# A fused attention and feed-forward kernel: turned blocks cross memory in one write and eight reads, fp8 steps walk rows with gaps, small vector operations go tile by tile

## The reference

```python
x = x + L0_xattn(layernorm(x), ctx)     # softmax((ctx Wq + bq)(ctx Wk + bk)^T), applied to x
x = x + L0_ffn(layernorm(x))            # rms norm, int8 activations, ternary weights, silu gate
x = x + L1_xattn(layernorm(x), ctx)     # 16 heads, 8 key heads; softmax(q k^T / sqrt(128)) v, then Wo
x = x + L1_ffn(layernorm(x))            # weights rounded to fp8 e4m3, silu gate, scales
```

## Time and profile before

| | |
|---|---|
| median of three runs | 310.96 us |
| the profiled execution | 312.58 us |
| its span, first to last instruction | 310.5 us |
| granted TensorE clock, mean share | 0.995 |
| PE / DVE / ACT / POOL busy | 95% / 84% / 82% / 70% |
| transfers | 44.59 MB, 144 GB/s on average |

### The profile page before, as it was taken

One profiled execution on the slowest core, in us unless ns is written; L12 is line 12 of the kernel. 1 busy time (PEld: TensorE's weight loads), 2 busy tenths in 40 slices (PEclk: granted clock), 3 DMA queues, 4 the chain that ended last, 5 costly groups with the idle time before them and its releaser, 6 DMA issues.

```text
span 310.5 us, 6396 instructions
## 1 busy us (share of the span) xinstructions
PE 293.6 (95%) x1980; PEld 259.9 (84%) x1992; DVE 260.9 (84%) x713; ACT 253.7 (82%) x603; POOL 218.5 (70%) x290
## 2 busy tenths in 40 slices
PE   3968999999999999999999999999999999999994
PEld 2755487798989998979889999999988999899884
DVE  3959999999999999889999986997768897675665
ACT  2398995598999998979999899778899999855460
POOL 3558864556998578999879998886678798952001
PEclk9979999999999999999999999999999999999999
DMA  7996032001326548885878756537645647200103
GB/s 223 367 381 199 35 101 70 1 8 30 93 47 189 157 138 251 220 212 139 228 210 226 199 144 174 161 108 219 182 144 148 179 143 211 68 3 0 36 1 101
DMA packets 54609, 44.59 MB, mean 144 GB/s; under 512 B 11696, under 2 KB 45104, under 8 KB 54576
## 3 DMA queue, kind: packets, MB, share of 16 engines
q1 hardware_dynamic: 54016, 43.93, 49.0%
q10 hardware_dynamic: 560, 0.26, 0.3%
HBM read 27.01 MB, written 15.20 MB: 136 GB/s over the span
## 4 chain that ended last, share of the span: by engine, by line
PE 59%; DVE 20%; DMA 8%; issue 5%; SPq 4%; ACT 2%; DVEq 0%
PE pb L2016 41%; DMA block_room<-blocks 5%; PE pb L2279 5%; PE pb L2314 4%; DMA wraw<-in_wgvT 3%; DVE blocks L1581 3%; SPq L442 2%; DVE sm L1564 2%; PE pb L2130 2%; PE pb L2091 2%; PE pb L2076 2%; DVE wraw L1455 2%; DVE step L1601 1%; PE pb L2227 1%; DVE q_lo L1551 1%
## 5 line engine op out<-in xcount | busy, mean ns | idle before, releaser
L667 POOL TENSOR_TENSOR tp_lo<-tp,pT_hi 128x512 fp32r<-128x512 f32 x54 | 70.0, 1311 | 15.1 <-ACT pT_hi L993 14.8
L981 ACT ACTIVATE sm<-sm,smin 128x256 f32<-128x256 f32 x128 | 63.6, 501 | 4.7 <-DVE smin L1564 4.4
L1564 DVE CUSTOM_DVE_ANT_0 sm<-pb,mask_all 128x256 f32<-128x256 f32 x128 | 47.3, 418 | 5.6 <-PE pb L2016 5.5
L1581 DVE STREAM_TRANSPOSE blocks<-sm 128x1024 f32<-128x1024 f32 x27 | 33.5, 1240 | 7.4 <-DMA block_room<-blocks 7.0
L2016 PE MATMUL pb<-ctx_hi,q_hi 128*128 128x256 f32 x128 | 38.1, 298 | 1.1 <-DVE q_lo L1551 0.6
L662 POOL TENSOR_SCALAR sm<-sm,srec 128x256 f32<-128x256 f32 x64 | 30.5, 488 | 10.4 <-DVE srec L1570 10.4
L2016 PE MATMUL pb<-xT_hi,m_hi 128*128 128x256 f32 x128 | 37.3, 292 | 0.3 <-DVE xT_lo L1540 0.3
L2016 PE MATMUL pb<-n_hi,oT_hi 128*128 128x256 f32 x128 | 37.1, 290 | 0.2 <-DVE oT_lo L1595 0.2
L2016 PE MATMUL pb<-xT_hi,m_lo 128*128 128x256 f32 x128 | 36.2, 283 | 0.0
L2016 PE MATMUL pb<-xT_lo,m_hi 128*128 128x256 f32 x128 | 36.2, 283 | 0.0
L2016 PE MATMUL pb<-ctx_lo,q_hi 128*128 128x256 f32 x128 | 36.2, 282 | 0.0
(11 more groups left out here) (195 smaller groups left out, 943.0 us busy)
## 6 DMA issues: line engine op xcount, KB each, us to landing
block_room<-blocks SPq DMA_DIRECT2D x108, 128.0 KB, 2.8
tp<-block_room SPq DMA_DIRECT2D x54, 256.0 KB, 3.0
w_raw<-in_w SPq DMA_DIRECT2D x4, 576.0 KB, 4.6
wraw<-in_wgvT SPq DMA_DIRECT2D x4, 512.0 KB, 8.4
wraw<-in_woutT SPq DMA_DIRECT2D x2, 512.0 KB, 9.3
out<-xb SPq DMA_DIRECT2D x4, 256.0 KB, 2.2
xa<-in_x SPq DMA_DIRECT2D x3, 256.0 KB, 4.5
xb<-in_ctxT SPq DMA_DIRECT2D x2, 256.0 KB, 5.1
```

What stands on the lines that cost most here:

```text
L667: g.tensor_tensor(tp_lo[:, z, c, :], tp[:, z, c, :], as_f32(pT_hi[:, c, :]), ALU.subtract).then_inc(pT_lo_pool, 1)
L981: a.activation(sm[:, n % 2, k, :], sm[:, n % 2, k, :], ACT.Exp, bias=smin[:, n % 2, k:k + 1], scale=-1.0, accum_out=ssum[:, n % 2, k:k + 1 ...
L1564: v.tensor_tensor_reduce(out=sm[:, n % 2, k, :], in0=bank(passing_bank("s", 2 * n + h))[:, (k % 2) * S:(k % 2 + 1) * S], in1=mask_all[:, b ...
L1581: v.transpose(blocks[:].rearrange("p g k b -> p k g b"), sm[:, n % 2, :, :].rearrange("p k (g b) -> p k g b", b=32)).then_inc(blocks_done, 1)
```

## The change

One DMA now writes all of `blocks` to `block_room` as it lies, 128 partitions with 4 KB each, in place of four DMAs that regrouped it on the way out in runs of 512 bytes. Regrouping moves to the reads: eight DMAs of 32 partitions and runs of 512 bytes (four for each half of `tp`), in place of two of 128 partitions and runs of 2 KB. The counts of the semaphores follow. `sum8` becomes three rows of 96 in rows of 97, and all fp8 steps on both engines see their operands as three rows of 96; VectorE's first step writes into `sum8` and its second reads that. In `stats`, `variances`, `second_stats` and `scaled` the 128x2 instructions become two of 128x1, and two products of tensors become a product with a per-row scalar.

```diff
-        sum8 = tile(ctx, "sum8", [P, PIECE])[:]
+        sum8 = tile(ctx, "sum8", [P, 3, PIECE // 3 + 1])[:, :, 0:PIECE // 3]
...
-        block_room = nc.dram_tensor("block_room", [2 * S, 2 * TOK], F32).ap()
+        block_room = nc.dram_tensor("block_room", [2, P, S * 2 * TOK // P], F32).ap()
...
+        def thirds(piece):
+            return piece.rearrange("p (a n) -> p a n", a=3)
...
-                    sp.wait_ge(blocks_in[0], 16 * (k - 1))
-                    sp.wait_ge(blocks_in[1], 16 * (k - 1))
-                rows = block_room[k % 2 * S:(k % 2 + 1) * S, :].rearrange("(g a) e -> a g e", a=32)
-                for i in range(4):
-                    sp.dma_start(rows[:, :, i * P:(i + 1) * P], blocks[32 * i:32 * (i + 1), :, :, :].rearrange("a g k b -> a g (k b)")).then_inc(blocks_out, 16)
+                    sp.wait_ge(blocks_in[0], 64 * (k - 1))
+                    sp.wait_ge(blocks_in[1], 64 * (k - 1))
+                sp.dma_start(block_room[k % 2], blocks[:].rearrange("p g k b -> p (g k b)")).then_inc(blocks_out, 16)
...
-                sp.wait_ge(blocks_out, 64 * (k + 1))
+                sp.wait_ge(blocks_out, 16 * (k + 1))
+                room = block_room[k % 2].rearrange("(i a) (c g e) -> a c g i e", a=32, c=SC, e=P)
                 for c in range(SC):
                     if k >= 1:
-                        sp.wait_ge(blocks_in[c], 16 * k)
-                    sp.dma_start(tp[:, k % 2, c, :], block_room[k % 2 * S + c * P:k % 2 * S + (c + 1) * P, :]).then_inc(blocks_in[c], 16)
+                        sp.wait_ge(blocks_in[c], 64 * k)
+                    for q in range(4):
+                        sp.dma_start(tp[32 * q:32 * (q + 1), k % 2, c, :].rearrange("a (i e) -> a i e", e=P), room[:, c, q, :, :]).then_inc(blocks_in[c], 16)
...
-                v.tensor_scalar(nmean[:, sl], mv[:, sl, 0], -1.0, None, ALU.mult)
+                for t in range(sl.start, sl.stop):
+                    v.tensor_scalar(nmean[:, t:t + 1], mv[:, t, 0:1], -1.0, None, ALU.mult)
...
-                scale_next(v.tensor_tensor(hmax[:, sl], hmax[:, sl], rstd[:, 1, sl], ALU.mult))
-                scale_next(v.tensor_scalar(hstep[:, sl], hmax[:, sl], EPS, 1.0 / 127.0, ALU.max, ALU.mult))
+                each = [slice(t, t + 1) for t in range(sl.start, sl.stop)]
+                for one in each:
+                    scale_part(v.tensor_scalar(hmax[:, one], hmax[:, one], rstd[:, 1, one], EPS, ALU.mult, ALU.max))
+                dve.wait_ge(scale_step, scale_count[0])
+                for one in each:
+                    scale_part(v.tensor_scalar(hstep[:, one], hmax[:, one], 1.0 / 127.0, None, ALU.mult))
+                dve.wait_ge(scale_step, scale_count[0])
                 scale_next(v.reciprocal(hrec[:, sl], hstep[:, sl]))
-                scale_next(v.tensor_tensor(hqs[:, sl], hrec[:, sl], rstd[:, 1, sl], ALU.mult))
+                for one in each:
+                    scale_part(v.tensor_scalar(hqs[:, one], hrec[:, one], rstd[:, 1, one], None, ALU.mult))
+                dve.wait_ge(scale_step, scale_count[0])
...
-                v.tensor_scalar(step8.bitcast(I32), w8_raw[:, n * PIECE:(n + 1) * PIECE].bitcast(I32), 0x7F800000, None,
+                v.tensor_scalar(sum8.bitcast(I32), thirds(w8_raw[:, n * PIECE:(n + 1) * PIECE]).bitcast(I32), 0x7F800000, None,
                                 ALU.bitwise_and).then_inc(exp8_done, 1)
                 dve.wait_ge(exp8_done, 2 * n + 1)
-                v.tensor_scalar(step8, step8, FP8_LEAST, FP8_STEP, ALU.max, ALU.mult).then_inc(exp8_done, 1)
+                v.tensor_scalar(thirds(step8), sum8, FP8_LEAST, FP8_STEP, ALU.max, ALU.mult).then_inc(exp8_done, 1)
```

More of the change, by code:

```diff
@@ L669, in eighths @@
             def eighths(n):
-                raw = w8_raw[:, n * PIECE:(n + 1) * PIECE]
+                raw = thirds(w8_raw[:, n * PIECE:(n + 1) * PIECE])
                 pool.wait_ge(exp8_done, 2 * n + 2)
-                g.tensor_tensor(sum8, raw, step8, ALU.add).then_inc(sum8_done, 1)
+                g.tensor_tensor(sum8, raw, thirds(step8), ALU.add).then_inc(sum8_done, 1)
             def eighths_out(n):
                 pool.wait_ge(sum8_done, n + 1)
-                g.tensor_tensor(sum8, sum8, step8, ALU.subtract).then_inc(step8_done, 1)
+                g.tensor_tensor(sum8, sum8, thirds(step8), ALU.subtract).then_inc(step8_done, 1)
                 pool.wait_ge(step8_done, 2 * n + 1)
-                g.tensor_scalar(step8, sum8, FP8_OVER, 0.0, ALU.mult, ALU.mult).then_inc(step8_done, 1)
+                g.tensor_scalar(thirds(step8), sum8, FP8_OVER, 0.0, ALU.mult, ALU.mult).then_inc(step8_done, 1)
                 pool.wait_ge(step8_done, 2 * n + 2)
-                g.tensor_tensor(w8r[:, n * PIECE:(n + 1) * PIECE], sum8, step8, ALU.add).then_inc(w8_done, 1)
+                g.tensor_tensor(thirds(w8r[:, n * PIECE:(n + 1) * PIECE]), sum8, thirds(step8), ALU.add).then_inc(w8_done, 1)
             def rows4(b):
@@ L985, in probs @@
                 if by_blocks(n):
-                    act.wait_ge(blocks_in[c], 16 * (turns_before(n) + 1))
+                    act.wait_ge(blocks_in[c], 64 * (turns_before(n) + 1))
                     whole = tp[:, turned_room(n), c, :]
@@ L1409, in stats @@
                 dve.wait_ge(mv_done, bn_count[0])
-                v.tensor_scalar(nmean[:, sl], mv[:, sl, 0], -1.0, None, ALU.mult)
+                for t in range(sl.start, sl.stop):
+                    v.tensor_scalar(nmean[:, t:t + 1], mv[:, t, 0:1], -1.0, None, ALU.mult)
             def variances(sl, done):
-                v.tensor_scalar(ve[:, 0, sl], mv[:, sl, 1], EPS, None, ALU.add).then_inc(done, 1)
+                for t in range(sl.start, sl.stop):
+                    ins = v.tensor_scalar(ve[:, 0, t:t + 1], mv[:, t, 1:2], EPS, None, ALU.add)
+                ins.then_inc(done, 1)
             def stats1(b):
@@ L1460, in second_stats @@
                 stats(xa, sl)
-                v.tensor_scalar(ve[:, 0, sl], mv[:, sl, 1], EPS, None, ALU.add)
-                v.tensor_scalar(ve[:, 1, sl], mv[:, sl, 1], 1.0 + EPS, EPS * EPS, ALU.mult, ALU.add).then_inc(ve2_done, 1)
+                for t in range(sl.start, sl.stop):
+                    v.tensor_scalar(ve[:, 0, t:t + 1], mv[:, t, 1:2], EPS, None, ALU.add)
+                    ins = v.tensor_scalar(ve[:, 1, t:t + 1], mv[:, t, 1:2], 1.0 + EPS, EPS * EPS, ALU.mult, ALU.add)
+                ins.then_inc(ve2_done, 1)
             def centred(b):
@@ L1478, in _, with scale_part, scale_next @@
             scale_count = [0]
-            def scale_next(ins):
+            def scale_part(ins):
                 scale_count[0] += 1
                 ins.then_inc(scale_step, 1)
+            def scale_next(ins):
+                scale_part(ins)
                 dve.wait_ge(scale_step, scale_count[0])
@@ L1488, in scaled @@
                 dve.wait_ge(rstd2_done, b + 1)
-                scale_next(v.tensor_tensor(hmax[:, sl], hmax[:, sl], rstd[:, 1, sl], ALU.mult))
-                scale_next(v.tensor_scalar(hstep[:, sl], hmax[:, sl], EPS, 1.0 / 127.0, ALU.max, ALU.mult))
+                each = [slice(t, t + 1) for t in range(sl.start, sl.stop)]
[5 more added lines that the diff above has]
+                dve.wait_ge(scale_step, scale_count[0])
                 scale_next(v.reciprocal(hrec[:, sl], hstep[:, sl]))
-                scale_next(v.tensor_tensor(hqs[:, sl], hrec[:, sl], rstd[:, 1, sl], ALU.mult))
+                for one in each:
+                    scale_part(v.tensor_scalar(hqs[:, one], hrec[:, one], rstd[:, 1, one], None, ALU.mult))
+                dve.wait_ge(scale_step, scale_count[0])
                 if b == 0:
                     dve.wait_ge(wmean_done, 1)
-                v.tensor_scalar(gsc[:, sl], hstep[:, sl], wmean[:, 0:1], None, ALU.mult).then_inc(gsc_done, 1)
+                for one in each:
+                    ins = v.tensor_scalar(gsc[:, one], hstep[:, one], wmean[:, 0:1], None, ALU.mult)
+                ins.then_inc(gsc_done, 1)
                 for t in range(TB):
@@ L1577, in turn_blocks @@
                 if k >= 1:
-                    dve.wait_ge(blocks_out, 64 * k)
+                    dve.wait_ge(blocks_out, 16 * k)
                 elif n >= 1:
@@ L1589, in probs_low @@
                 if n == LAST_TURNED + 1 and c == 0:
-                    dve.wait_ge(blocks_out, 64 * turns_before(n))
+                    dve.wait_ge(blocks_out, 16 * turns_before(n))
                 v.tensor_tensor(pT_lo[:, c, :], bank(passing_bank("pT", SC * n + c)), as_f32(pT_hi[:, c, :]), ALU.subtract).then_inc(pT_lo_done, 1)
```

## The result

The change makes the kernel slower: 329.51 us median (329.41 to 330.29) against 311.27 for the kernel before in the same comparison, a ratio of 1.056 with an interval of 1.052 to 1.060. The forecast was 312.3 us with a range to 317.0; the measured time lies 12.5 us above that range. Of the three outcomes, slower had been given 0.33.

The account below looks back on a forecast made before the run. TensorE, 95% busy, was taken as the bound, with VectorE and SP's queue next to it. Small operations +1.0, fp8 steps -1.7 and the stall +2.0 made +1.3 us: 312.3 us on the median's scale, range 307.9 to 317.

Parts of the forecast that it names:

- The write: Single 512 KB store of the blocks on SP's queue: lands after 3.0 us, 1.3 us shorter than the four issues.
- The reads: Eight read issues a turn keep SP 3.55 us; the halves of `tp` are there after 3.5 and 5.3 us.
- The fp8 steps: Rows of 96 no longer wait for GpSimd, 0.45 us a step; TensorE regains 1.7 us, bounds 0 and 2.55.
- the loop: SP's turn of write, landing and reads grows from 5.2 to 6.7 us, against 6.47 between turns: a lack of 0.2.
- I count it at nothing: Turns 4 to 20: queue up to 3.5 us behind, mostly covered by the shorter write and slack, so no loss.
- about 1.2 us a turn: Slack in SP's loop: its waits for VectorE, 28.2 us in 23 waits.
- rival (c): SP's queue tight from turn 12 on, loop 7.25 us, turn 29 5.5 us late, 315.8 us in all; chance 0.23.
- Where two writes stand side by side it catches up: In SP's queue, delay from turns of write, read, write, read is made up at adjacent writes, except at the end.
- The last turns: From the reads of turn 21 to the end, SP's queue falls behind and TensorE stalls about 2.0 us.
- The small operations: Split statistics instructions from 20 to 76 us: 2.0 us more on VectorE, TensorE 1.0 us late, bounds 0 and 2.0.

Follow-up runs that it names:

- e3: Kernel before with only the fp8 steps on rows of 96 in rows of 97; 314.45 us against 313.12, ratio 1.004.
- e4: Kernel before with only the small operations split by tiles; 313.38 us against 313.12, ratio 1.002.
- e5: Changed kernel with two plain reads a turn in place of eight, blocks not regrouped; 307.21 us against 311.83 for before, ratio 0.987.
- e10: Kernel before with one write, two plain reads a turn (blocks not regrouped) and fp8 rows of 96; 307.21 us against 312.69, ratio 0.986.
- e1: Kernel before with only the transfers of the change, one write and eight reads a turn; 329.37 us against 313.12, ratio 1.053.
- e2: Changed kernel with the transfers of before, so only fp8 rows and small operations remain; 314.71 us against 313.12 for before, ratio 1.007.
- e8: Changed kernel with the next turn's write issued between the reads of the two halves, same transfers; 311.79 us against 311.83 for before, ratio 0.998.
- e9: Kernel before with one write and two plain reads a turn, blocks not regrouped; 309.89 us against 312.69, ratio 0.993.
- e14: Kernel before with fp8 rows of 96 and 480 more unused bytes, so later tiles move by 512; 309.38 us against 312.31, ratio 0.992.
- e16: Kernel before with one write, two plain reads (not regrouped), fp8 rows of 96, later tiles moved by 512 bytes; 307.96 us against 312.31, ratio 0.986.
- e13: Kernel before with 32 unused bytes per partition behind the fp8 tiles, moving later tiles; 314.27 us against 312.31, ratio 1.006.
- e15: Kernel before with one write, two plain reads (not regrouped) and 32 unused bytes moving later tiles; 309.84 us against 312.31, ratio 0.994.
- e6: Changed kernel with two plain reads (not regrouped), then six 1 KB DRAM-to-DRAM transfers a turn; 349.76 us, ratio 1.121 to before.

## Why the prediction was wrong

**What held.** That TensorE is the bound and that SP's loop stands next to it. The write: 3.0 us forecast, 2.9 at the median, 3.1 on average over the turns. The reads: 3.55 us of SP forecast, 3.62 where nothing disturbs them; the halves of `tp` there after 3.5 and 5.3, measured 3.5 and 5.65 at the median. The fp8 steps at 0.45 us without long ones: 0.443 and 0.453. The Trainium skill's "VectorE: DVE Perf Modes", What auto-detection actually checks, said that rows of three would drop out of the two-port mode; the trace agrees, with 450 and 455 ns as the longest where 1472 and 1448 stood. The other page cited, "DMA: Bandwidth & Descriptors" of the Trainium skill, Anatomy of one DMA, gave an estimate of 3.2 and 2.15 us for write and read; 2.9 and 2.1 were measured. Small reads did turn out to be dear, but by their issues on SP and not by their landings.

**The step that failed first: "the loop".** 6.7 us a turn was made of undisturbed issues and a typical landing; 7.17 were measured. In the profile after, a turn's reads keep SP 3.94 us on average, where 3.55 were forecast and 3.62 is the least, since single issues take long (up to 2.04 us against 0.43). Writes land after 3.11 on average, where 3.0 were forecast and 2.7 is the least; four of the 27 take 3.9 to 4.7. In a loop that hardly anything outside holds back, there is no place where such a delay is made up, so the mean counts and not the median: 26 x 0.47 = 12 us. The forecast's loop has no term for what else SP's queue carries. The latest landing is that of a write behind which the queue issued a transpose by DMA of other data (start us, us, what):

```profile
170.11 4.71 DMA block_room<-blocks
170.57 2.74 SPq L434 DMA_TRANSPOSE uqT<-uq  x1
```

The next latest, 4.44 us, has such a transpose behind it as well; that these delay the landing is not shown by a run of its own, and why single issues take long stays open. An undisturbed turn, as turn 26 with 6.53 us, is hardly above the spacing of before, so nearly all of the loss came in disturbed turns.

**The step that failed second: "I count it at nothing".** A loop 0.2 us longer than the spacing of turns, as forecast, had to be paid in all 26 turns, 6 us. I started the count at turn 21, whose reads "start at 213.96, held by TensorE", and left turns 4 to 20 to slack. But TensorE's time at that place is itself a result of the loop: its reads started at 224.74, 10.8 us later. The writes of turns 4, 12 and 21, before and then after (start us, us, what), show how the loss grows from the start:

```profile
97.75 2.53 SPq L442 DMA_DIRECT2D block_room<-blocks  x4
148.82 1.82 SPq L442 DMA_DIRECT2D block_room<-blocks  x4
209.00 1.84 SPq L442 DMA_DIRECT2D block_room<-blocks  x4
97.83 0.43 SPq L443 DMA_DIRECT2D block_room<-blocks  x1
155.41 0.36 SPq L443 DMA_DIRECT2D block_room<-blocks  x1
219.85 0.34 SPq L443 DMA_DIRECT2D block_room<-blocks  x1
```

The later three are 0.1, 6.6 and 10.9 us behind the earlier three. The slack of "about 1.2 us a turn" was also a little less: 28.2 us in 23 waits is 1.2 a wait, and 1.04 over 27 turns. For the same reason rival (c) had the right loop, 7.25, and the wrong price, 5.5 in place of 26 x (7.25 - 6.47) = 20.

**"Where two writes stand side by side it catches up"** was wrong as well. There is one tile `blocks`, so the second write waits for the first to land and for a transpose of 1.25: from 243.44 to 256.53, two turns take 13.1 us, where the forecast's own times had 12.05 (230.95 to 243.0) and before 2 x 6.47 = 12.9. Of SP's 12.9 us of waits for VectorE 7.7 stand at the three such places.

**The last turns.** 2.0 us were forecast from the reads of turn 21 to the end. In the profile after, the reads of turns 21 and 29 start at:

```profile
224.74 0.30 SPq L458
280.25 3.63 SPq L458 DMA_DIRECT2D tp<-block_room  x8
```

That is 10.8 and 15.9 us late, against 213.96 and 264.38, and the end is 17.0 late. So 6.2 us came in where 2.0 were forecast: here the size was wrong as well, by the same disturbed turns.

**The fp8 steps.** 1.7 us were forecast; by itself the gain of the rows is 2.9 (interval 1.5 to 3.7 by the ratio), a little over the bound of 2.55 that I took from TensorE's idle time. What the term left out is the move of later tiles, +2.0 with the writes of before. How the two combine there is not settled: their medians add to a gain of 0.9, and e3, which has both, was 1.3 slower; the intervals reach 1.1 us to either side in each. In the changed kernel neither decides, since the queue sets the pace.

**The small operations.** + 1.0 us was forecast; e4 shows + 0.3 with -0.4 to + 1.6 by the ratio, and e5 and e10, which differ by them, stand at 0.987 and 0.986 in their comparisons. No loss is shown.

**The sum** of e1 (+16.3) and e2 (+1.6) is 17.9, against 18.2 for the change.

## What to carry to other kernels

Where one queue issues, waits for a landing and issues again once per turn, add up its turn and compare it with the turn of the bound engine: each tenth of a microsecond too much is paid in every turn, means count and not medians, and a moment at which another engine holds the queue today must not be taken as fixed. Saving three issues ahead of a landing for six more behind it lengthens such a loop even where each single transfer lands sooner; putting other work of the queue between an issue and its landing (e8) takes the loss away without touching a transfer. A tile that grows by a few bytes moves all that are allocated behind it, so a change of layout should be tried with the old places kept.

## What the runs showed of the hardware beyond that

A move of tiles by 32 bytes changes both TensorE's pace and transfers. Over the 128x256 products of the attention that follow each other within 140 ns (some 1,060), the mean distance of starts is 119.5 to 119.6 ns in before, e4, e9, e14 and e16 and 118.6 to 118.8 in after, e3, e10, e13 and e15: the kernels whose tiles stand 32 bytes off are about 0.9 us quicker there. The 27,904 packets of 512 bytes have the same median, 27 ns, but a tenth of them take 47 ns or more in e2, e3 and e13, against 41 in before, e4 and e14, and the four-part write lands 4.6 to 4.8 us after its first issue (medians over the turns) against 4.4 to 4.5. The Trainium skill's "DMA: Bandwidth & Descriptors", How a descriptor splits into AXI transactions, says that a piece of a transfer which does not start at a multiple of 256 bytes costs extra beats of 32 bytes. By the addresses of the tiles, `blocks` starts 128 bytes behind such a multiple in before and 160 in the kernels with the move, so an estimate by that page is 20 beats for a run of 512 bytes before and 21 after, and one more in 132 for a run of 4 KB. The trace agrees in the direction, and in that the single write with 4 KB runs shows nothing (2.85 us in e1, 2.86 in the changed kernel); packets that take 47 ns in place of 41 show more than one beat in twenty. No run here varies the offset further.

The time that SP needs for an issue does not follow the bytes: 0.36 us for a 512 KB write, 0.43 for a 64 KB read, 0.59 for 1 KB from DRAM to DRAM (medians of the issues in after and e6).
